# First layer with the condition as the stationary operand, its result turned afterwards; the second weight matrix loaded from ScalarE's queue

## What is computed

```python
h = silu(cond @ W1.T + b1)                 # 128 x 512
gate = sigmoid(h @ W2.T + b2)[:, None, :]  # one row for each sample
# a Haar transform over the steps, every coefficient times gate, and its inverse
a = inverse_haar(gate * haar(x))
out = x + (x + a)
```

## Time and profile before

| | us |
|---|---|
| median of 3 runs | 167.27 |
| the profiled execution's own time | 167.46 |
| its span (first to last instruction) | 165.7 |
| what lies around the span | 1.76 |
| DVE busy | 79.5 |
| PE busy | 25.9 |
| ACT busy | 2.5 |

### The profile page before, as it was taken

One profiled execution on the slowest core, in us unless ns is written; L12 is line 12 of the kernel. 1 busy time (PEld: TensorE's weight loads), 2 busy tenths in 40 slices (PEclk: granted clock), 3 DMA queues, 4 the chain that ended last, 5 costly groups with the idle time before them and its releaser, 6 DMA issues.

```text
span 165.7 us, 270 instructions
## 1 busy us (share of the span) xinstructions
PE 25.9 (16%) x94; PEld 18.7 (11%) x94; DVE 79.5 (48%) x19; ACT 2.5 (1%) x3; POOL 2.6 (2%) x10
## 2 busy tenths in 40 slices
PE   0679999800000000000000000000000000000000
PEld 0668883300000000000000000000000000000000
DVE  0250082499999999500099992000000599960000
ACT  3000010100000000000000000000000000000000
POOL 6000000000000000000000000000000000000000
PEclk9996559995555555555555555555555555555555
DMA  5989969997997979998997999899899989899994
GB/s 171 556 350 506 490 285 490 506 431 332 490 490 301 443 332 475 490 395 380 506 459 332 475 490 395 380 506 459 364 443 490 395 380 506 364 419 427 427 451 190
DMA packets 1733, 69.49 MB, mean 419 GB/s; under 512 B 194, under 2 KB 194, under 8 KB 324
## 3 DMA queue, kind: packets, MB, share of 16 engines
q1 hardware_dynamic: 1008, 35.91, 51.1%
q10 hardware_dynamic: 724, 33.56, 46.8%
HBM read 35.92 MB, written 33.55 MB: 419 GB/s over the span
## 4 chain that ended last, share of the span: by engine, by line
DMA 51%; DVE 16%; PE 16%; DVEq 5%; issue 0%; ACT 0%
DMA ring<-in_x 26%; DMA out<-ring 22%; DVE ring L228 10%; DVE ring L233 5%; DVEq L30 5%; PE hidden_sum L148 4%; DMA ring<-in_L_cond_W 3%; PE turned L173 2%; PE turned L131 2%; PE gate_sum L165 2%; PE turned L157 2%; PE hidden_sum L146 2%; PE gate_sum L161 1%; PE turned_cond L136 1%; DVE factor L223 0%; DVE ring L208 0%
## 5 line engine op out<-in xcount | busy, mean ns | idle before, releaser
L228 DVE TENSOR_TENSOR ring<-ring,factor 128x16384 f32<-128x16384 f32 x3 | 51.6, 17223 | 14.6 <-DMA ring<-in_x 14.6
L233 DVE TENSOR_TENSOR ring<-ring,factor 128x8192 f32<-128x8192 f32 x2 | 17.3, 8689 | 30.2 <-DMA ring<-in_x 30.2
L148 PE MATMUL hidden_sum<-ring 128*128 128x128 f32 x32 | 7.0, 386 | 0.0
L205 DVE COPY ring<-turned 128x512 f32<-128x512 f32 x4 | 2.8, 692 | 7.4 <-PE turned L131 7.4
L148 PEld LDWEIGHTS hidden_sum<-ring 128*128 128x128 f32 x32 | 5.9, 276 | 0.7 <-issue 0.4
L211 DVE TENSOR_TENSOR ring<-hidden_sum,ring 128x512 f32<-128x512 f32 x1 | 0.7, 692 | 10.4 <-ACT ring L181 10.4
L223 DVE TENSOR_SCALAR factor<-turned 128x512 f32<-128x512 f32 x4 | 2.8, 692 | 5.5 <-PE turned L173 5.5
L131 PE MATMUL turned<-identity,ring 128*128 128x128 f32 x16 | 3.6, 423 | 5.8 <-DMA ring<-in_L_cond_W 5.8
L131 PEld LDWEIGHTS turned<-identity,ring 128*128 128x128 f32 x16 | 3.3, 228 | 5.8 <-issue 5.8
L215 DVE COPY ring<-turned 128x512 f32<-128x512 f32 x4 | 3.8, 1072 | 0.0
L173 PE MATMUL turned<-ring 128*128 128x512 f32 x8 | 3.7, 602 | 0.8 <-ACT ring L184 0.8
(11 more groups left out here) (14 smaller groups left out, 5.1 us busy)
## 6 DMA issues: line engine op xcount, KB each, us to landing
out<-ring ACTq DMA_DIRECT2D x2, 4096.0 KB, 16.9
ring<-in_L_cond_W SPq DMA_DIRECT2D x2, 1024.0 KB, 6.1
ring<-in_cond SPq DMA_DIRECT2D x1, 256.0 KB, 5.1
ring<-in_x SPq DMA_DIRECT2D x4, 44.2
out<-ring ACTq DMA_DIRECT2D x3, 45.6
b_row<-in_L_cond_b ACTq DMA_DIRECT2D x2, 2.0 KB
```

Of the source, the lines that this page charges most:

```text
L148: last = pe.matmul(block_of(hidden_sum, t), block_of(w1_t[:, c, :], t), block_of(cond_t, c), start=False, stop=(c == BLOCKS - 1))
L228: dve.tensor_tensor(ring[:, c, :, :], ring[:, c, :, :], steps_of(c, STEPS), ALU.mult).then_inc(chunk_scaled, 1)
L233: dve.tensor_tensor(ring[:, 0, piece(h), :], ring[:, 0, piece(h), :], steps_of(CHUNKS - 1, PIECE), ALU.mult).then_inc(chunk_scaled, 1)
```

## The change

The first layer is computed the other way round: the turned condition is the stationary operand and the turned weights stream past it in 512 columns. Its result has samples in its partitions, so four more transposes and one more DVE copy turn it for the second layer. The load of `W2` goes from third place on SP's queue to first place on ACT's, ahead of the two bias rows.

```diff
         def _(sp):
             sp.dma_start(w1_rows, w1.rearrange("(p t) k -> p t k", t=BLOCKS)).then_inc(w1_loaded, DMA_DONE)
             sp.dma_start(cond_rows, cond).then_inc(cond_loaded, DMA_DONE)
-            sp.dma_start(w2_rows, w2.rearrange("(p m) k -> p m k", m=BLOCKS)).then_inc(w2_loaded, DMA_DONE)
...
-            b1_strided = b1_row[:, :].rearrange("a (p t) -> a t p", t=BLOCKS)
             pe.wait_ge(ones_set, 1)
             pe.wait_ge(b1_loaded, DMA_DONE)
-            pe.wait_ge(w1_t_set, BLOCKS)
+            pe.matmul(hidden_sum[:, :], ones_row[:, :], b1_row[:, :].rearrange("a (p t) -> a t p", t=BLOCKS),
+                      start=True, stop=False)
             pe.wait_ge(cond_t_set, 1)
-            for t in range(BLOCKS):
-                pe.matmul(block_of(hidden_sum, t), b1_strided[:, t, :], ones_row[:, :], start=True, stop=False)
-                for c in range(BLOCKS):
-                    last = pe.matmul(block_of(hidden_sum, t), block_of(w1_t[:, c, :], t), block_of(cond_t, c),
-                                     start=False, stop=(c == BLOCKS - 1))
+            for c in range(BLOCKS):
+                pe.wait_ge(w1_t_set, c + 1)
+                last = pe.matmul(hidden_sum[:, :], block_of(cond_t, c), w1_t[:, c, :],
+                                 start=False, stop=(c == BLOCKS - 1))
             last.then_inc(hidden_summed, 1)
...
+            pe.wait_ge(hidden_set, 1)
+            for t in range(BLOCKS):
+                last = pe.transpose(block_of(turned_hidden, t), block_of(hidden, t), identity[:, :])
+            last.then_inc(hidden_turned, 1)
+
             pe.wait_ge(b2_loaded, DMA_DONE)
             pe.matmul(gate_sum[:, :], ones_row[:, :], b2_row[:, :], start=True, stop=False)
-            pe.wait_ge(hidden_set, 1)
+            pe.wait_ge(hidden_t_set, 1)
             for t in range(BLOCKS):
                 pe.wait_ge(w2_t_set, t + 1)
-                last = pe.matmul(gate_sum[:, :], block_of(hidden, t), w2_t[:, t, :],
+                last = pe.matmul(gate_sum[:, :], block_of(hidden_t, t), w2_t[:, t, :],
                                  start=False, stop=(t == BLOCKS - 1))
...
         def _(act):
+            act.dma_start(w2_rows, w2.rearrange("(p m) k -> p m k", m=BLOCKS)).then_inc(w2_loaded, DMA_DONE)
             act.dma_start(b1_row[:, :], b1.rearrange("(a j) -> a j", a=1)).then_inc(b1_loaded, DMA_DONE)
...
             for t in range(BLOCKS):
+                if t == BLOCKS - 1:
+                    dve.wait_ge(hidden_turned, 1)
+                    dve.tensor_copy(hidden_t, turned_hidden[:, :]).then_inc(hidden_t_set, 1)
                 dve.wait_ge(w2_turned, t + 1)
```

More of the change, by code:

```diff
@@ L56, in gated_residual_program @@
         hidden = ring[:, SCRATCH, 19, :]
-        gate = ring[:, SCRATCH, 20, :]
-        spread = ring[:, SCRATCH, 21:21 + GROUPS, 0:P]
+        hidden_t = ring[:, SCRATCH, 20, :]
+        gate = ring[:, SCRATCH, 21, :]
+        spread = ring[:, SCRATCH, 22:22 + GROUPS, 0:P]
         turned = [psum(f"turned{c}", [P, D]) for c in range(BLOCKS)]
@@ L62, in gated_residual_program @@
         hidden_sum = psum("hidden_sum", [P, D])
+        turned_hidden = psum("turned_hidden", [P, D])
         gate_sum = psum("gate_sum", [P, D])
@@ L71, in gated_residual_program @@
         hidden_summed, sigmoid_set, hidden_set = sem("hidden_summed"), sem("sigmoid_set"), sem("hidden_set")
+        hidden_turned, hidden_t_set = sem("hidden_turned"), sem("hidden_t_set")
         ones_spread, lower_set, spread_set = sem("ones_spread"), sem("lower_set"), sem("spread_set")
```

## The result

The changed kernel takes 166.91 us (median of 20 runs, 166.47 to 167.85), the kernel before 167.99 us (20 runs, 166.93 to 169.3). The ratio is 0.9933 with a 95% interval of 0.991 to 0.9956: 0.7% faster. So the likeliest case was the wrong one, and what happened, by the gain of 1.1 us, is the rival "the ends give more than 0.5 us", which had 7.

What follows compares the result with a forecast made beforehand. The prediction took the DMA engines, never idle from 4 to 164 us, as the bound. From 167.27 us, 0 for the gate and -0.1 for the ends gave 167.2 us, range 166.4 to 168.0.

Steps and rivals of the forecast that it cites:

- the likeliest case: Whole kernel: no change because the DMA engines are never idle, 166.7 to 167.7 us; 81 in 100.
- the ends give more than 0.5 us: Rival at start and end: instruction load or fuller start comes out near its bound, 165.8 to 166.7 us; 7 in 100.
- What bounds the kernel: From 4 to 164 us the DMA engines are never out of work, share 1.00 at 430 GB/s; bytes over rate plus ends.
- The slack: How late the gate may be: 13.0 us for chunk 2's load, 12.2 us for chunk 0's store, at no cost.
- late limit of 46.4: Chunk 2's load must be issued by 46.4 us, 2.4 us before chunk 1 lands at 48.8.
- At every moment there is work for all engines: Middle of the kernel: bytes are the same and queues never empty, so the gate's time adds 0 us.
- The sum for the gate: Start of the first big multiply: 34.12 + 2.44 - 5.68 + 0.87 = 31.8 us, bounds 29.3 and 35.4.
- W1's delay: At the start, W2's load shares the DMA engines with W1's, so W1 lands 2.44 us later, near 8.1.
- the full clock: First layer: eight passes of 512 columns priced at 3.65 us, like L165; the layer ends 5.68 us earlier.
- The extra DVE copy: Before the second layer: 0.70 us, ahead of the last W2 copy, taken as hidden under the bias of 1.11 us.
- The change doesn't do what it says: Rival: the gate is no earlier or some microseconds later, yet the time stays 167.2 us; 25 in 100.
- The ends: Fuller start (0 to -0.49 us) and instruction load gone (0 or -0.96), together taken as -0.1 us.

Runs made afterwards that it cites:

- change_long_program: The changed kernel with 16 extra 8-column matmuls on PE behind the gate's last matmul, results unused; 167.92 us against 168.15 for the kernel before, ratio 0.9991.
- the queue alone: The kernel before with only W2's load moved to first place on ACT's queue, first layer unchanged; 167.87 us against 168.15, ratio 0.999.
- the last pair: The changed kernel with two idle DVE multiplies ahead of the hidden product, without and with 16 extra PE matmuls (the long one); 166.74 and 168.36 us.
- the first layer alone: The changed kernel with W2's load kept third on SP's queue, so only the first layer differs from before; 167.25 us against 168.15, ratio 0.9967.
- before_short_gate_late: The kernel before with twelve first-layer matmuls left out and two idle DVE multiplies making the gate late again; 167.25 us against 167.8, ratio 0.9963.

## Why the prediction was right and wrong

**What bounds the kernel: right.** The DMA share is 1.00 and the rate 430 GB/s between 4 and 164 us before and after, and the gate can move from a store issued at 48 to one at 62 us without a difference that can be told.

**The slack: right above, blind below.** The late limit of 46.4 predicted 9.0 us of loss for a load issued at 55.4, and 9.9 were measured. That an early gate could cost anything I had not thought of. "At every moment there is work for all engines" was true in that case too (share 0.98), but it leaves out that a packet can take longer: 367 GB/s with full queues. What must be constant is share and rate. The kernel before, with its store at 51.4, is some 5 us from that edge (45.6 was slow, 48.1 was not). The changed kernel is further away, at 54.0, and neither the time of the change nor that of before rests on it as far as these runs tell.

**The sum for the gate: wrong by 5 us, without consequence.** Predicted 31.8 (29.3 to 35.4), measured 36.77. W1's delay was as forecast: it lands at 8.17 (predicted 8.1). By the page on DMA (the Trainium skill, DMA: Bandwidth & Descriptors, Queues, rings and completion order) the engines go round their queues, and this trace agrees: W1's load took 7.37 us instead of 4.86, and between 3 and 7 us `q1` and `q10` moved 102 packets each. The step that failed is the price of the first layer at "the full clock": its eight passes took 6.56 us, not 3.65, and the bias 2.07, not 1.11. The second layer took 5.41, not 3.65. The upper bound of 35.4 was passed because it held a low clock for the eight passes of the first layer alone. The price also differs between executions: with the same first layer, change_long_program took 3.65 us for the eight passes, and its multiply started at 33.77. The extra DVE copy was not covered either: L171 starts at 26.16, when the copy L223 is done, though the bias L167 ended near 24.8. I had covered the copy by the bias, but it also queues behind three copies of W2, which come later than PE's turns when PE is fast. "The change doesn't do what it says" (25 in 100) is what happened: the gate is later, and it cost nothing.

**The ends: the step that decided, and was mis-sized.** I priced them at -0.1 us with a bound of -1.45, "nearer to 0 because the other fifteen engines keep their work". That reason is the error. The end is a maximum over sixteen engines, so fifteen that keep their work don't soften the delay of the one. The load cost that engine its own 1.03 us, and the next packet on it was longer too. Transfers of 35.7 to 35.8 us of the kernel before:

```profile
q1 hardware_dynamic: 1, 0.07, 182.2%
```

One 64 KB packet with 182.2% of 1.6 us is 2.92 us, half a microsecond over the usual 2.42. So a load of instructions costs up to 1.5 us on its engine, less what the sixteen engines differ by anyway. The comparisons gave 0.6 to 1.6 us.

**That the time lies in the range is luck.** The sum started from 167.27 us, the median of three runs of the kernel before. Over twenty runs that median is 167.99, which is 0.72 higher. The gain of 1.08 us taken off 167.27 gives 166.2, below the range's end of 166.4. So the gain was mis-sized by 1 us, and a start that was 0.7 us low hid most of it.

**What stays open.** Why the queue alone showed no packet in its profile: the load may be missing in some executions, and the wide spread of the long programs (before from 166.77 to 169.3) would fit, but I didn't show it. What makes one engine late without a load, and why the last pair differs by 1.3 to 1.6 us, about all that the load and the packet behind it can cost (in the long one's trace the late engine also has a packet of 4.25 us at 62.9). Whether the 0.3% between the first layer alone and the full change is the queue's, the long packets of the mixed stretch or chance: the intervals overlap. And by what mechanism a store and a load slow each other when they start together: that it is their timing is shown by before_short_gate_late, the cause of the longer packets was not tried.

## What to carry to other kernels

Where the DMA engines are the bound, compare them one by one at the end: a transfer is as late as its slowest engine, and a lone packet for something else (here 16 KB of instructions, gone once PE's program was shorter) can decide when it falls to that engine. Before work on a chain that waits somewhere in the middle, compute by when it must be ready; outside of that it buys nothing, and readiness that is too early can start a store beside a load at a bad moment. Judge such a stretch by its rate and not by its busy share.

## What the hardware showed unexpectedly

- A store and a load of 8.39 MB each that started together ran at 367 GB/s, with a DMA share of 0.98, against 419 (before_short_gate_late) and 421 GB/s (before) over the same 50 to 90 us with the store issued 5 to 6 us later.
- A load of 16 KB of instructions took a DMA engine 1.03 us, though 64 KB of data take it 2.42, and lengthened the packet behind it by 0.5, in three traces alike.
- The view of the granted clock didn't tell PE's speed at the start. These are stretches of the changed kernel; the granted clock is the third number from the end:

```profile
14.90:21.40 6.50, 6.50 (x10) 2.74 (x11) 0.00 (x0) 0.00 (x0) 0.00 (x0) 1.00 1.12 484
21.40:23.50 2.10, 2.10 (x20) 2.10 (x19) 1.40 (x2) 0.60 (x1) 0.00 (x0) 1.00 1.15 499
27.60:31.50 3.90, 3.90 (x6) 1.30 (x4) 0.00 (x0) 0.00 (x0) 0.00 (x0) 0.57 0.93 403
```

  All of the first two stretches stand at 1.00 (2.4 GHz). But the passes of 512 columns in the first took 0.82 us each (6.56 / 8), against 0.46 for L165 before (3.65 / 8). The records of single passes say more. In the first stretch seven of eight last 0.91 us or more, mostly 1.06, like the 1.05 to 1.06 of L171's passes from 27.55 us on, where the granted clock is at the lower level of 1.2 GHz. At 2.4 GHz the same passes last 0.59. The trace's first record of the clock begins at 20.72 us, and for time without a record the view shows 1.00. The eighth pass, begun at 20.84, lasted 0.59. PE had been at work since 8.31 by then, and the sixteen transposes behind, in the second stretch, took 2.1 us against 3.65 at the start. In the kernel before, the transposes of W1 (L131) last 0.42 us each, exactly as long as those of W2 (L157) under a granted 0.50; W2's last 0.28 in the second stretch above. The same holds for every trace of this case: PE works at its slow rate until the first record begins. So the 1.00 ahead of it is no measurement. My price of "full clock" came from L165, which ran under a recorded 1.00, and could not be carried over to 15 us.
